# Three of eight heads transposed by the DMA in place of two, and new-value requests joined, in a paged attention kernel

## The reference

```
x = x + einsum('bct,bcd->bdt', x, weights[subjects])
q, k, v = x @ Wq.T, x @ Wk.T, x @ Wv.T            # 32 query heads, 8 key/value heads of 128
q, k = rope(rmsnorm(q) * q_norm_w), rope(rmsnorm(k) * k_norm_w)     # positions start at cache_seqlens
k_all = concat(k_cache[block_table], k)           # 16 pages x 32 keys = 512 old keys, 32 new keys
v_all = concat(v_cache[block_table], v)
probs = softmax(where(valid, q @ k_all.T / sqrt(128), -1e30))
x = x + (probs @ v_all) @ Wo.T
```

## Time and profile before

| | |
|---|---|
| times of three runs | 1025.1, 1018.34, 1021.69 us, median 1021.69 |
| the profiled execution | its span is 1018.6 us; a time of its own beside it is not given, and the fastest run's is 1018.34 |
| TensorE busy | 965.9 us, 95% of the span |
| VectorE, ScalarE, GpSimd busy | 821.1, 738.2, 536.8 us |
| transfers | 294.89 MB, 290 GB/s over the span; SyncE's queue 74.6% of the DMA engines' time, GpSimd's 17.6% |
| granted TensorE clock | full in all forty slices |

### The profile page before, as it was taken

One profiled execution on the slowest core, in us unless ns is written; L12 is line 12 of the kernel. 1 busy time (PEld: TensorE's weight loads), 2 busy tenths in 40 slices (PEclk: granted clock), 3 DMA queues, 4 the chain that ended last, 5 costly groups with the idle time before them and its releaser, 6 DMA issues.

```text
span 1018.6 us, 24766 instructions
## 1 busy us (share of the span) xinstructions
PE 965.9 (95%) x8097; PEld 799.2 (78%) x8097; DVE 821.1 (81%) x1755; ACT 738.2 (72%) x2007; POOL 536.8 (53%) x706
## 2 busy tenths in 40 slices
PE   4889999999889988899999999999999999989998
PEld 2668888888677777787788888888888888878885
DVE  6779999999998688878877777877787787877770
ACT  4888999988784687877767676767676776767660
POOL 4445565655893057655555464455445544544440
PEclk9999999999999999999999999999999999999999
DMA  5789999989997979999999998999998999999950
GB/s 197 252 271 319 326 391 362 386 294 381 393 350 250 377 268 330 357 280 249 258 301 284 275 292 280 312 264 284 321 278 258 317 296 251 311 279 288 265 125 11
DMA packets 249903, 294.89 MB, mean 290 GB/s; under 512 B 79024, under 2 KB 206512, under 8 KB 247216
## 3 DMA queue, kind: packets, MB, share of 16 engines
q1 hardware_dynamic: 231088, 226.07, 74.6%
q0 software_dynamic: 18688, 67.25, 17.6%
HBM read 231.77 MB, written 46.27 MB: 273 GB/s over the span
## 4 chain that ended last, share of the span: by engine, by line
PE 69%; DVE 14%; issue 6%; ACT 5%; POOL 3%; DMA 1%; SPq 1%; DVEq 0%; ACTq 0%; POOLq 0%
PE ps_proj L1465 16%; PE ps_y L1465 15%; PE ps_o L1540 13%; PE ps_s L1503 7%; PE ps_t L1514 7%; PE ps_s L1507 6%; PE ps_rt L1611 2%; DVE c_stage L1361 2%; DVE rot L1333 2%; DVE probs L1209 2%; DVE stage L1347 1%; PE ps_t L1522 1%; PE ps_o L1552 1%; DVE rot L1325 1%; POOL probs L920 1%
## 5 line engine op out<-in xcount | busy, mean ns | idle before, releaser
L920 POOL TENSOR_SCALAR probs<-probs,recip 128x544 f32<-128x544 f32 (+1 forms) x256 | 162.4, 635 | 298.0 <-DVE recip L1217 290.8
L994 ACT ACTIVATE probs<-probs,neg_max 128x544 f32<-128x544 f32 x256 | 191.5, 748 | 148.9 <-DVE neg_max L1209 132.5
L1209 DVE CUSTOM_DVE_ANT_0 probs<-ps_s,mask,row_scale 128x544 f32<-128x544 f32 x256 | 200.4, 783 | 65.9 <-PE ps_s L1507 50.0
L1540 PE MATMUL ps_o<-pt,vs 128*128 128x128 f16 x3072 | 213.3, 219 | 0.5 <-DMA vs<-v_pages,v_row 0.5
L1540 PEld LDWEIGHTS ps_o<-pt,vs 128*128 128x128 f16 x3072 | 192.7, 98 | 14.9 <-DMA vs<-v_pages,v_row 0.9
L874 POOL TENSOR_TENSOR roped<-rot 128x256 f32<-128x256 f32 x160 | 144.2, 923 | 81.2 <-DVE rot L1325 78.1
L1229 DVE SCALAR_TENSOR_TENSOR pt<-ps_t,pt 128x512 f16<-128x512 f32 x190 | 130.0, 684 | 48.7 <-ACT pt L1000 42.7
L1465 PE MATMUL ps_proj<-wt_hi,x0t_hi 128*128 128x512 f32 x384 | 159.6, 416 | 7.4 <-DVE x0t_lo L1167 6.4
L1465 PE MATMUL ps_y<-wo,ot_hi 128*128 128x512 f16 x512 | 153.5, 381 | 2.6 <-DVE ot_lo L1241 2.6
L1465 PE MATMUL ps_proj<-wt_hi,x0t_lo 128*128 128x512 f32 x384 | 151.8, 395 | 0.0
L1465 PE MATMUL ps_proj<-wt_lo,x0t_hi 128*128 128x512 f32 x384 | 150.8, 393 | 0.0
(11 more groups left out here) (153 smaller groups left out, 1644.0 us busy)
## 6 DMA issues: line engine op xcount, KB each, us to landing
kt<-k_pages_t SPq DMA_DIRECT2D x512, 128.0 KB
c_nat<-in_L_cond_k_cache SPq DMA_DIRECT2D x32, 512.0 KB, 6.0
q_t<-stage SPq DMA_DIRECT2D x64, 256.0 KB, 6.8
c_nat<-in_L_cond_v_cache SPq DMA_DIRECT2D x32, 512.0 KB, 7.2
qt<-q_t SPq DMA_DIRECT2D x32, 512.0 KB
w_nat<-in_L_cond_Wq SPq DMA_DIRECT2D x8, 1024.0 KB, 8.7
k_pages_t<-c_stage SPq DMA_DIRECT2D x16, 512.0 KB, 5.8
c_nat<-in_L_cond_Wo SPq DMA_DIRECT2D x16, 512.0 KB, 7.5
```

Source lines behind the costliest of these rows:

```text
L920: pool.tensor_scalar(part, part, col(recip, i), 1.0, ALU.mult, ALU.mult).then_inc(p_norm, 1)
L994: act.activation(pr, pr, ACT.Exp, bias=col(neg_max, i), scale=-1.0, accum_out=col(row_sum, i)).then_inc(a_exp, 1)
L1209: dve.tensor_tensor_reduce(out=probs_of(i), in0=ps_s[:, score_cols(i):score_cols(i) + KEYS], in1=mask[(i // HK) % 2][:, mask_at(i):mask_at ...
L1540: ins = pe.matmul(ps_o[n % 2][:, jl * P:(jl + 1) * P], v[:, part, :], pt[pt_slot(i)][:, NCH * half + c, :], start=jl == 1 and c == 0 and k ...
```

## The change

Four things:

- `by_dma` takes h0, h3 and h4 of each batch (`DMA_HEADS = (0, 3, 4)`), still from head 24 on. So h3 is turned by the DMA, in the batches 3 to 31. VectorE's `t_lo`, which in the last step of a unit stands early, is left out there.
- `weighed` has an order for each unit of a batch: 1, 2, 0, 3 for h0 to h3, and 1, 2, 3, 0 for h4 to h7 as before. h0 is weighed a step earlier, h3 a step later.
- `pt_free`, which keeps a slot of `pt` from being written before it has been weighed, waits for one more head at h7. SyncE issues the transposition of h3 right behind that of h0.
- The new values of a batch come by two requests in place of three: the high part, which is stored twice, is one request of 64 partitions that reads its source twice; the low part is a second. The semaphore counts to 32 per batch in place of 48.

```diff
--- before.py
+++ after.py
@@ -434,10 +434,12 @@
 
     TN, TNE, TNC, OE = HPC - 1, HPC, HPC, HPC + 3
     DMA_FIRST, T_THIRD = 24, 24
+    DMA_HEADS = (0, 3, 4)
+    ORDERS = ((1, 2, 0, 3), (1, 2, 3, 0))
 
     def by_dma(i):
 
-        return DMA_FIRST <= i < NP2 and i % HPC == 0
+        return DMA_FIRST <= i < NP2 and i % HK in DMA_HEADS
 
     def dma_no(i):
 
@@ -459,12 +461,12 @@
     def pt_free(eng, i):
 
         if i > HPC:
-            eng.wait_ge(t_pv, i - HPC)
+            eng.wait_ge(t_pv, i - HPC + (i % HK == HPC + 3))
 
     def weighed(m):
 
         n, r = divmod(m, HPC)
-        return HPC * n + (r + 1) % HPC
+        return HPC * n + ORDERS[n % 2][r]
 
     def split_rows(i, part):
 
@@ -703,9 +705,10 @@
                 s = b % 2
                 if b >= 2:
                     sp.wait_ge(t_pvn, NHALF * (b - 1))
-                for j in range(3):
-                    part = (0, 0, 1)[j]
-                    sp.dma_start(vn[s][SEQ * j:SEQ * (j + 1)], v_new[b][:, part]).then_inc(d_vn[s], 16)
+                high, low = (v_new[b][:, part].rearrange("t j d -> t (j d)") for part in range(2))
+                sp.dma_start(vn[s][0:2 * SEQ].rearrange("p j d -> p (j d)"),
+                             high.rearrange("(a t) f -> a t f", a=1).to_broadcast((2, SEQ, HK * D))).then_inc(d_vn[s], 16)
+                sp.dma_start(vn[s][2 * SEQ:3 * SEQ].rearrange("p j d -> p (j d)"), low).then_inc(d_vn[s], 16)
 
             def load_wo(k):
                 h0 = WO_LOAD * k
@@ -817,6 +820,7 @@
                     load_queries(b + 2)
                     load_pages(b + 2, 0, NPP)
                 turn_rows(HK * (b + 1))
+                turn_rows(HK * (b + 1) + 3)
                 if b + 2 < B:
                     load_new_v(b + 2)
                 for k in WO_WITH_KEYS.get(b + 1, ()):
@@ -941,7 +945,7 @@
                 if at(i, TNC) is not None:
                     tn_copy(at(i, TNC), min(i + 3, NP2))
                 if i == 0:
-                    pool.wait_ge(d_vn[0], 48)
+                    pool.wait_ge(d_vn[0], 32)
                 if late_head(i - 1) is not None and on_pool(late_head(i - 1)):
                     wo_low(late_head(i - 1))
                 if i == 0:
@@ -1441,7 +1445,7 @@
                     add_residual(y_out(i))
                 if by_dma(i + 2):
                     row_recip(i + 2)
-                if late_new(i):
+                if late_new(i) and not by_dma(i):
                     t_lo(i)
                 if i + AHEAD < NP2:
                     masked_max(i + AHEAD)
@@ -1544,7 +1548,7 @@
             def weigh_new(n):
                 b, h = divmod(n, NHALF)
                 if h == 0:
-                    pe.wait_ge(d_vn[b % 2], 48 * (b // 2 + 1))
+                    pe.wait_ge(d_vn[b % 2], 32 * (b // 2 + 1))
                 pe.wait_ge(p_tncopy, n + 1)
                 pe.wait_ge(v_tnlo, n + 1)
                 for jl in range(HPC):
```

## The result

The changed kernel takes **1089.29 us** in the median (1085.08 to 1104.4), against 1020.02 for the kernel before on the same chip: ratio 1.0648, 95% interval 1.0611 to 1.0686. It is slower by 66 to 69 us, where the forecast was 1068, and it lies in the forecast's range. (Disturbed executions are left out of every ratio here, so a ratio can stand a little beside that of the medians.) The profiled execution took 1086.27 us, its span is 1084.5; the kernel before had 1018.6.

What follows compares the result with a forecast made beforehand. TensorE was taken to bound the attention stage. The span of 1018.6 us, less 12.8, plus 59.6 gave 1065.4; with the runs' median 3.1 over the span, the forecast was 1068 us, range 1035 to 1100.

Steps and rivals of the forecast that it cites:

- TensorE's gain: On TensorE in the attention stage: 29 transpositions of h3 go, 0.44 us each, 12.8 us less.
- The split buffers: ScalarE's split of h4 waits for h0's DMA landing; TensorE's weighing of h2 waits 2.13 us, 28 times: 59.6 us more.
- ScalarE and VectorE's exchange: Evictions and splits change between these engines: +3.9 and +3.5 us in all, on engines with idle time, nothing by itself.
- SyncE: SyncE's issue queue: one more transposition, one request fewer per batch; 16.6 becomes 18.2 us of 19.65, still fits, nothing.
- The joined request: New values loaded by two requests in place of three, wanted sixteen heads later: costed at nothing.
- rival 2: Transfers land later: joined request on two engines, 2.7 us, half reaching h0's landing, 38 us more: 1106; chance 12%.
- Third transposition in the trough: DMA transfers: a third transposition per batch goes into the trough behind the first; nothing on the path.
- Rival 1: At h0's DMA landing: if within 4.55 us of issue, TensorE never waits and the gain stands: 1009 us; chance 7%.
- Rival 3: SyncE becomes the bound: with 2.5 us issues its batch is 18.5 of 19.65 - 0.44; not reached, no separate chance.

Runs made afterwards that it cites:

- less volume: The both repaired kernel with one of the four value gathers of each batch left out (its products use old values): 1005.97 us, ratio 0.9845.
- one-buffer kernel: The kernel before with one buffer of split rows in place of two, nothing else changed: 1152.97 us, ratio 1.1325.
- four corners: The change with two or three split buffers, and joined or three requests: ratios 1.0648 (two, joined), 1.0911 (three, joined), 1.0588 (two, three), 1.0093 (three, three).
- both repaired: The change with three split buffers (output weights' lead 1 in place of 2) and three requests for new values: 1031.91 us, ratio 1.0093.
- the control: The kernel before with three split buffers and the output weights' lead 1 in place of 2: 1024.5 us, ratio 1.0027.

## Why the prediction was right, and where its sizes were off

**TensorE's gain:** right, and hidden. With less volume the busy time is 952.5 us, where 965.9 - 12.8 = 953.1 was due.

**The split buffers:** right, in place, count and size. 28 waits of ScalarE on a transfer; TensorE stopped at h2's low half 27 times in the rows, for 60.9 us, against 59.6 forecast, and its idle time grew by 58.1. The one-buffer kernel shows the wait without the change's transfers, and the four corners show that its removal alone does not help. This last thing the prediction did not say; it costed each suspect as if the others were absent. That the total fits so closely is partly luck. In the mean of 28 batches h4's split starts 6.54 us after h0's issue (6.68 taken), the chain behind it takes 2.16 (2.33 taken), and TensorE wants h2 6.54 us after that issue, where 7.32 - 0.44 = 6.88 was taken: -0.14 - 0.17 + 0.34 cancel to 0.03.

**The mis-sized term** is the price of a pause. I made the sum in idle time and took every matmul at the duration of the kernel before. Behind eleven of the 23 pauses TensorE ran at 1.2 GHz (0.50) for a while; where this began at once, twelve matmuls took 1.46 us in place of 0.84. Measured: 20.6 us of busy time more. With it the sum -12.8 + 59.6 becomes +67.4, and the span of 1084.5 is +65.9. The mean wait of 2.13 us does not show this: the pauses spread up to 5.2 us, and those followed by the slow clock run from 1.96 to 5.17.

**ScalarE and VectorE's exchange:** no wait of its own shows up. From the end of the split's wait to the weighing all 27 pauses show 2.16 or 2.17 us, where 2.33 was taken.

**SyncE:** right for the change, whose batches have gaps ahead of the query load (642.95 + 0.37 to 644.81, 646.08 to 647.01). It is not so that h3's transposition follows h0's at once (659.8 in the prediction): SyncE waits for VectorE's rows, 80.6 us in 54 times where it was 2.1 in 3 before, and could afford it. Wrong once the waits are taken out: with both repaired its queue has hardly a gap. "It still fits" took the issues at their durations before (16.6 of 19.65 us), and these are not fixed. The sixteen page loads are issued in 9.00 us in the median before, 9.38 with both repaired and 11.15 where the joined request is in the way of three buffers; one transposition in 1.55, 2.11 and 2.25. As I read it, the issue time of a queue under load measures the transfers, not SyncE; less volume bears that out for the transpositions (1.30).

**The joined request:** "nothing" held nearly in the change (0.6%, not told from nothing), since it was hidden behind another wait, not because it is cheap. Two engines were shown, the price was the one worked out in rival 2 (65 KB on each at 24 GB/s, 2.7 us; 49 GB/s measured), but it did not reach h0's landing in the way that rival 2 said: those of the change read 5.3 to 8.2 us, those of before 5.5 to 8.9. It fell on the page loads and the transpositions instead, 8 per cent between the two kernels with three buffers (1118.24 and 1031.91 us). How two busy engines hold up transfers that need all sixteen is inferred from the 13.24 us, not shown.

**Third transposition in the trough:** "nothing on the path" holds for batches of 22.5 us (448.24 to 1010.76, 25 batches). For one of 19.5 it is false, as less volume shows: this alone would have turned the gain of 12.8 into a loss of some 7 (1031.91 against 1024.5 of the control).

**The rivals.** Rival 1 (cover holds) fell: the landings of h0 stay above 5 us. Rival 2 fell as told, and its cause came back elsewhere. Rival 3 was not reached, for a reason that it named itself: the wait makes the batch longer. Its own sum was wrong, though. From the query load to h0's transposition are 11.11 us, three issues of 2.5 are 7.5 and the two requests 0.85: 19.46 us, not 18.5, and so more than the 19.21 that it is held against. The both-repaired kernel, without that wait, is where this picture appears.

**A better version:** the third transposition in every second batch with three buffers and three requests, ratio 0.9971 (0.9945 to 0.9997), 4.1 us. That fits the terms: 15 x 0.44 = 6.6 less, 2.8 for the room made, 3.8 us. It is the best of the versions tried that still loads everything, and hardly more than the scatter of its runs.

## What to carry to other kernels

When a stage's order changes, write down for each rotating buffer who its previous user now is and what must land before it is free; the edit here never touched that buffer, and it decided. Before believing that a repair "didn't help", make the repairs together: two causes in the same place hide each other, and only the four corners told 5, 8 and 1 per cent apart. Cost a pause of TensorE not only by its length but by the granted clock of the microseconds behind it, and read the issue time of one transposition as a sign of how full the queue is, once the waits between two issues are taken out.

## What the runs showed that I had not expected

- A pause has a second price. In the changed kernel the granted clock fell to 0.50 behind eleven of the 23 pauses of TensorE over 1 us, of 1.96 to 5.17 us, and not behind two others of 2.98 and 3.54. With one buffer, 16 of 25 pauses (1.99 to 5.70 us) were followed at once by two matmuls in 0.60 or 0.61 in place of 0.38, two of them after pauses of only 2.33 and 2.44.
- Taking a wait away made the kernel slower: 1089 to 1118 us with a third buffer. As I read it, the wait had spaced the transfers; that was not tried by itself.
- A transposition issued earlier, amid the pages, landed later after its issue: h0's took 9.5 us in the median, against 6.6.
- One DMA transposition takes SyncE 1.23 us to issue at the least; the medians are 1.30 with less volume, 1.76 in the change and 2.11 with both repaired, and the most is 7.23 with three buffers and the joined request. It grows as the transfers fill up.
